# Attention of a two-layer transformer kernel: units of two heads in one sequence of ticks, scores 12 and 14 products behind the maxima

## The reference

```python
# layer 0 attention: 16 heads of 16, 4 key/value heads, band of +-64 tokens, a sink added to every score
att = einsum('bhqd,bhkd->bhqk', q, k) * 16 ** -0.5 + sink
att = softmax(where(|i - j| <= 64, att, -inf))
x = layernorm(x + (att @ v) @ wo)
x = layernorm(x + int8_ffn(x))                  # 256 -> 1024 -> 256
# layer 1 attention: 16 heads of 16, causal
att = softmax(where(j > i, -inf, q @ k.T * 0.25))
x = layernorm(x + (att @ v) @ w_out.T + b_out)
x = layernorm(x + moe(x))                       # 2 of 16 experts, and 2 shared ones
```

## Time and profile before

| what | us |
|---|---|
| median of 3 runs (lowest to highest) | 995.63 (992.62 to 998.64) |
| the profiled execution | 998.8 |
| its span, first to last instruction | 997.0 |
| PE busy | 827.6 (83%) |
| DVE, ACT, POOL busy | 555.6, 492.1, 348.5 |

### The profile page before, as it was taken

How to read it: one execution, slowest core, us unless ns; L and a number is a source line. 1 busy time by engine, 2 the same in 40 slices (tenths; PEclk the granted TensorE clock), 3 DMA queues, 4 the chain that set the end, 5 groups by cost and what they waited for, 6 DMA issues and landing times. The chain is left out here.

```text
span 997.0 us, 15493 instructions
## 1 busy us (share of the span) xinstructions
PE 827.6 (83%) x5521; PEld 641.7 (64%) x5534; DVE 555.6 (56%) x1381; ACT 492.1 (49%) x1064; POOL 348.5 (35%) x630
## 2 busy tenths in 40 slices
PE   6996999889789997988899889699984328999946
PEld 3775766577577566756756677477643318889935
DVE  5543478465337845814685473347825406688924
ACT  3373555745455475554447645355462106555503
POOL 6762502415341032344303326251141560045521
PEclk9697999979799997988999798799996658999978
DMA  8049000000000000000000000003323220045452
GB/s 225 2 26 247 1 1 2 2 1 24 1 1 1 2 2 1 3 23 0 1 2 2 1 2 2 1 1 136 127 52 80 74 99 20 17 139 155 139 201 84
DMA packets 34626, 47.27 MB, mean 47 GB/s; under 512 B 9948, under 2 KB 27998, under 8 KB 33688
## 3 DMA queue, kind: packets, MB, share of 16 engines
q1 hardware_dynamic: 25184, 20.29, 8.5%
q0 software_dynamic: 6656, 23.27, 7.3%
q10 hardware_dynamic: 2712, 2.73, 0.8%
HBM read 20.09 MB, written 18.69 MB: 39 GB/s over the span
## 5 line engine op out<-in xcount | busy, mean ns | idle before, releaser
L1033 DVE TENSOR_REDUCE negmax<-ps 128x2 fp32r<-128x512 f32 (+4 forms) x304 | 176.9, 628 | 45.0 <-PE ps L1347 42.5
L765 ACT ACTIVATE prob<-ps 128x448 f32<-128x448 f32 (+2 forms) x320 | 151.1, 524 | 57.5 <-PE ps L1360 55.0
L1347 PE MATMUL ps<-kT,qT 128*128 128x256 f32 (+4 forms) x512 | 150.8, 371 | 0.0
L1360 PE MATMUL ps<-qT,kT 128*128 128x192 f32 (+4 forms) x512 | 122.6, 328 | 10.2 <-ACT prob L765 4.7
L572 POOL TENSOR_TENSOR carry_p<-neg_half 128x1 f32<-128x1 f32 x80 | 16.4, 205 | 284.0 <-ACT prob L765 284.0
L1360 PEld LDWEIGHTS ps<-qT,kT 128*128 128x128 f32 x512 | 82.9, 198 | 47.3 <-ACT prob L765 32.5
L577 POOL TENSOR_SCALAR_AFFINE_SELECT prob<-prob 128x512 f32<-128x512 f32 (+1 forms) x192 | 110.1, 602 | 0.0
L1347 PEld LDWEIGHTS ps<-kT,qT 128*128 128x128 f32 x512 | 95.6, 200 | 3.0 <-issue 0.8
L1374 PE MATMUL ps<-prob,v_aug 128*32 128x256 f32 (+4 forms) x1024 | 77.7, 411 | 13.3 <-POOL prob L577 13.1
L902 DVE TENSOR_TENSOR xT<-ps,xT 128x256 fp32r<-128x256 f32 x96 | 39.4, 420 | 78.0 <-ACT xT L653 75.8
L616 POOL DMA_INDIRECT token_y<-ys_sb,y_row x47 | 45.1, 959 | 89.6 <-DVE ys_sb L1194 89.0
(11 more groups left out here) (206 smaller groups left out, 1835.8 us busy)
## 6 DMA issues: line engine op xcount, KB each, us to landing
xs_sb<-slot_x SPq DMA_DIRECT2D x47, 129.0 KB
slot_x<-zeros SPq DMA_DIRECT2D x1, 6016.0 KB, 33.2
w_sb<-in_w POOLq DMA_DIRECT2D x4, 1408.0 KB, 12.3
w_sb<-in_w POOLq DMA_DIRECT2D x5, 704.0 KB, 9.1
x_all<-in_x SPq DMA_DIRECT2D x4, 512.0 KB, 3.8
w_sb<-token_y SPq DMA_DIRECT2D x2, 1024.0 KB, 11.7
w_sb<-token_y ACTq DMA_DIRECT2D x2, 1024.0 KB, 12.6
out<-y_all SPq DMA_DIRECT2D x4, 512.0 KB, 2.9
```

The lines of the kernel that those rows point to most:

```text
L765: act.activation(prob[:, part % PROB_BUFS, j, 0:n], ps[:, 3 + i % 3, 0:n], ACT.Exp, scale=SCALE).then_inc(exped[l].sem, 1)
L1033: dve.tensor_reduce(out=negmax[:, t, s * GH + j * mh:s * GH + (j + 1) * mh], in_=ps[:, k % 3, 0:mh * n].rearrange("p (h n) -> p h n", n=n) ...
L1347: ins = pe.matmul(dst[:, jj, :], qT[:, h // 2, t * P:(t + 1) * P], kT[:, k_block(h), k0:k0 + n], start=False, stop=True, skip_group_check= ...
L1360: ins = pe.matmul(ps[:, 3 + item % 3, col:col + n], kT[:, k_block(h), kt * P:(kt + 1) * P], qT[:, h // 2, q0:q0 + n], start=True, stop=Tru ...
```

## The change

A unit of two heads (`UH = 2`, eight units) takes the place of the group of four. There are no slots: one sequence of ticks runs through the stage, and every step has the tick at which it stands worked out by a small function. Score item i stands at tick i + 12 in layer 0 and i + 14 in layer 1 (`SCORE_LAG`). The stage has 45 and 63 ticks instead of 48 and 72 places. Raw items are now 4 and 6 for a unit, so 32 and 48 for a stage: in layer 1 the item of four heads by 128 keys becomes two. The maxima are turned and sent once for a unit (8 times and not 4), and one DMA on SP carries both rows of a unit where two DMAs carried the four rows of a group. `pv_part` now has two heads and stands 6 score items back for odd units and 8 for even ones, so that the last part of an even unit and the first of the odd unit behind it have the same tick; the two units use different quarters of bank 6 (`c = 32 * (h % GH)`). `prob` has six buffers of two heads and not three of four, which is the same memory. `oT_copy`, `o_transposes` and `normalise` still go by four heads. POOL has 16 or 24 parts of two heads. The router input (`x3_tr`) stands at ticks 4 and 8, the router at tick 34, and the head steps of the next sequence at ticks 50, 52, ... 60.

The diff, cut to its core:

```diff
-PROB_BUFS = 3
+PROB_BUFS = 6
 PV_LAG = 6
 SHIFT_AT = 2
-MAX_HEADS = tuple([min(GH, 512 // query_tile_keys(l, t)[1]) for t in range(NT)] for l in (0, 1))
-MAX_ITEMS = tuple([(t, j) for t in range(NT) for j in range(GH // MAX_HEADS[l][t])] for l in (0, 1))
+NU, UH = 8, 2
+MAX_HEADS = tuple([min(UH, 512 // query_tile_keys(l, t)[1]) for t in range(NT)] for l in (0, 1))
+MAX_ITEMS = tuple([(t, j) for t in range(NT) for j in range(UH // MAX_HEADS[l][t])] for l in (0, 1))
+SCORE_LAG = (12, 14)
+X3_TICKS = (4, 8)
+def shift_tick(l, u):
+    return (u + 1) * len(MAX_ITEMS[l]) + SHIFT_AT
+def pv_tick(l, part):
+    n_parts = len(PARTS[l])
+    return UH * part + 1 + SCORE_LAG[l] + (PV_LAG if part // n_parts % 2 else PV_LAG + 2)
+def group_tick(l, g):
+    return pv_tick(l, (2 * g + 2) * len(PARTS[l]) - 1)
+def o_tick(l, g):
+    return group_tick(l, g) + (3, 4)[l]
+def head_tick(i):
+    return shift_tick(1, NU - 1) + 2 * i
+TICKS = tuple(NU * len(MAX_ITEMS[l]) + SCORE_LAG[l] + 1 for l in (0, 1))
...
-                        for parity in (0, 1):
-                            sp.dma_start(qT[STACK * parity + SHIFT:STACK * parity + SHIFT + 1, 2 * g:2 * g + 2, :].bitcast(F32),
-                                         shift_row[parity:GH:2, g % 2, :].bitcast(F32)).then_inc(sh_row[g][l].sem, 16)
+                        sp.dma_start(qT[SHIFT:P:STACK, u, :].bitcast(F32), shift_row[:, u % 2, :].bitcast(F32)).then_inc(sh_row[u][l].sem, 16)
...
-                                                             pattern=[[0, GH], [sign, hi_q - lo_q]], channel_multiplier=-sign)
+                                                         pattern=[[0, UH], [sign, hi_q - lo_q]], channel_multiplier=-sign)
...
-                    def pv_part(g, p):
-                        pe.wait_ge(*kept[l].at(b, g * n_parts + p + 1))
-                        if p == 0 and g >= 1:
-                            pe.wait_ge(*oT_out[l].at(b, g))
+                    def pv_part(part):
+                        u, p = divmod(part, n_parts)
+                        pe.wait_ge(*kept[l].at(b, part + 1))
+                        if p == 0 and u % 2 == 0 and u >= 2:
+                            pe.wait_ge(*oT_out[l].at(b, u // 2))
                         for i, (kt, off) in enumerate(PARTS[l][p]):
                             q0, n = key_tile_queries(l, kt)
-                            for j in range(GH):
-                                h = g * GH + j
-                                ins = pe.matmul(ps[32 * j:32 * j + 32, 6, q0:q0 + n],
+                            for j in range(UH):
+                                h = u * UH + j
+                                c = 32 * (h % GH)
+                                ins = pe.matmul(ps[c:c + 32, 6, q0:q0 + n],
...
-                            ins = pe.matmul(ps[0:GH, 7, t * P:(t + 1) * P], negmax[:, t, (s - 1) * GH:s * GH], ident_r[:],
+                            ins = pe.matmul(ps[0:UH, 7, t * P:(t + 1) * P], negmax[:, t, u * UH:(u + 1) * UH], ident_r[:],
...
-                    for s in range(NG + 2):
-                        g = s - 2
-                        if g >= 0:
-                            pe.wait_ge(*sh_row[g][l].at(b, 2 * 16))
-                        for i in range(max(n_items, n_parts * GH)):
-                            if g >= 0 and i < n_parts * GH:
-                                score_item(g, i)
-                            if s < NG and i < n_items:
-                                raw_item(s, i)
-                            if i == SHIFT_AT and 1 <= s <= NG:
-                                shift_tr(s)
+                    for k in range(TICKS[l]):
+                        if 0 <= k - SCORE_LAG[l] < NU * UH * n_parts:
+                            score_item(k - SCORE_LAG[l])
+                        if k < NU * n_items:
+                            raw_item(k)
+                        for u in range(NU):
+                            if k == shift_tick(l, u):
+                                shift_tr(u)
...
+                        for part in range(NU * n_parts):
+                            if k == pv_tick(l, part):
+                                pv_part(part)
+                        for g in range(NG - 1):
+                            if k == o_tick(l, g):
+                                o_transposes(g)
```

More of the change, by code:

```diff
@@ L217, in build @@
         scope.append(attn_scope)
-        prob = sb("prob", [P, PROB_BUFS, GH, 512])
+        prob = sb("prob", [P, PROB_BUFS, UH, 512])
         qkv_sb = sb("qkv_sb", [P, 6 * C])
@@ new lines, in batch @@
+                    n_parts = len(PARTS[l])
+                    for part in range(NU * n_parts):
+                        u, p = divmod(part, n_parts)
+                        buf = part % PROB_BUFS
+                        pool.wait_ge(*exped[l].at(b, (part + 1) * UH))
+                        c = (l * NU + u) * 3 + p
+                        pool.tensor_tensor(out=carry_p[:, c:c + 1], in0=neg_half[:], in1=neg_half[:], op=ALU.add)
+                        for kt, col in PARTS[l][p]:
+                            q0, n = key_tile_queries(l, kt)
+                            for lo_q, hi_q, base, sign in unseen(l, kt):
+                                sel = prob[:, buf, :, col + lo_q - q0:col + hi_q - q0]
+                                ins = pool.affine_select(out=sel, in_=sel, compare_op=ALU.is_ge, fill=0.0, base=base,
+                                                         pattern=[[0, UH], [sign, hi_q - lo_q]], channel_multiplier=-sign)
+                        ins.then_inc(kept[l].sem, 1)
+                        if l == 1 and not last:
+                            for i in range(HEAD_STEPS):
+                                if (head_tick(i) - SCORE_LAG[1]) // UH == part:
+                                    head_step(b + 1, i)
@@ new lines, in attention @@
+                    for k in range(TICKS[l] + 2):
+                        if k < NU * n_items:
+                            max_item(k)
+                        if l == 0 and b >= 1:
+                            for i in (0, 1):
+                                if k == X3_TICKS[i] + 1:
+                                    for t in (2 * i, 2 * i + 1):
+                                        split_lo(b - 1, "x3", t, bank0=4)
+                        for g in range(NG - 1):
+                            if k == o_tick(l, g) + 1:
+                                normalise(g)
+                        if l == 1 and not last:
+                            for i in range(HEAD_STEPS):
+                                if k == head_tick(i):
+                                    head_step(b + 1, i)
@@ L1383, in o_transposes @@
                             pe.wait_ge(*o_put[l].at(b, g))
+                        pe.wait_ge(*sh_out[l].at(b, sum(shift_tick(l, u) <= o_tick(l, g) for u in range(NU))))
                         for t in range(NT):
@@ L1441, in attention @@
+                    for part in range(NU * n_parts):
+                        if pv_tick(l, part) >= TICKS[l]:
+                            pv_part(part)
                     ahead = l == 1 and not last
```

201 lines of the change are left out of this document (87 added, 114 removed).

## The result

The median is **1026.26 us** (1024.95 to 1029.08) where the kernel before has 995.63: a ratio of 1.0305, 95% interval 1.0265 to 1.0345. The forecast was 1018, range 988 to 1042, own range 1008 to 1028. The profiled execution has a span of 1023.5 us (before 997.0), 26.5 more, where the sum said 22. PE's total and its main line come first; the columns of the group are busy us, mean ns, idle before and what ended it.

What follows compares the result with a forecast made beforehand. PE was taken to bound each attention stage's middle, and nearly its end. Layer 0's +4.6 and layer 1's +18 were rounded to +22 us: 998.8 profiled becomes 1021, median 1018; range 988 to 1042, own range 1008 to 1028.

Steps and rivals of the forecast that it cites:

- rival 4: Order tighter than its signals (bank 7, layer 1 row's DMA, POOL at the end): 1 to 2 us more a stage, 1030; chance 0.13.
- A pair costs what four cost: Value products on PE: two heads by 512 columns take 1.00 us, as four did; the line's 77.7 us about doubles.
- Rival 2: Every `pv_part`: a pair costs half of what four cost, so value products add nothing; 980 us, chance 0.10.
- Neighbours in one tick overlap: Even unit's last value part and odd unit's first: the shorter is hidden, 0.89 us a group in layer 0, 0.57 in layer 1.
- rival 1: Neighbouring value parts don't overlap: 23 us on top, 1041 us; chance 0.20.
- First part: Stage start with only raw items: shorter, 7.3 us (-2.4) in layer 0 and 7.2 us (-4.4) in layer 1.
- Third part and tail: Stage end: free PE time gained, 3.0 us in layer 1 and 3.2 in layer 0, less 0.8 there for a new wait.
- Rival 3: Gaps in the second and third parts are worth 1.5 to 2.5 us a stage more: about 1000 us; chance 0.20.
- The normalise wait at tick 30: Layer 0: the turning at tick 30 writes bank 7 and must wait for DVE's maximum 29 and `normalise`: 0.8 us.
- Router stages: Three layer 0 stages: -1.2 us for the first score's wait, +1.0 for less PE slack at a lower clock; +1.1 each in all.
- Layer 1, +5.1 a stage: Layer 1 stage sum: value products +8.0, turnings +0.7, first part -4.4, moved raw items +3.8, third part and tail -3.0 us.
- 4.5 as the mean of four: Layer 1's last stage has a first part 0.9 us longer but less free time at its end: mean 4.5 us, +18 in all.

Runs made afterwards that it cites:

- quads: Kernel after, with even units' value parts held back to the odd neighbour's so four heads stream together, 4 not 6 items behind in layer 1: 1000.63 us.
- own_tick: Kernel after, with all value parts of even units one tick earlier, so neighbouring units' parts don't share a tick: 1050.05 us.
- x3_before_late: Kernel before, with the router input's products between items of the first two slots and the expert weights' load after the last scores: 993.61 us.
- late_after: Kernel after, with the expert weights' load of the last sequence moved behind the last stage's scores: 1019.42 us.
- late_before: Kernel before, with the expert weights' load of the last sequence moved behind the last stage's scores: 993.91 us.

## Why the prediction was right, and where its size was off

The mechanism was right and with it the direction. The time came 8 us beyond the forecast, within its own range, but nearer to the 1030 of rival 4 than to 1018; and the 8 us are a sum of errors that partly cancel.

- **A pair costs what four cost.** Right: 0.99 us for a part, 122.7 us for the line (about 120). Rival 2 is gone by the trace, and quads shows it is the cause: 25.6 us come back.
- **Neighbours in one tick overlap.** Right: 1.00 us for both, and separated they cost +23.8 us where rival 1 put 23. That the two numbers meet is partly luck: 3.3 us of it are the new wait in layer 0, and the stages account for 19.8 us only.
- **Turnings.** 0.24 each, right.
- **First part.** In layer 1 6.68 where I had 7.2: -4.9 for -4.4, and no wait of 0.3 in the first seven stages. Layer 0: 6.8 for 7.3, so -2.9 for -2.4.
- **Third part and tail.** The 3.0 us that I took for layer 1 were free time of PE. Its visible idle there fell from 22.10 - 19.66 = 2.4 to 19.22 - 19.01 = 0.2 us; what short gaps gave besides can't be read. The lengths of the parts don't test the term, since ten score items moved from the third part into the middle. Rival 3 wanted 1.5 to 2.5 us more a stage, and the stages are longer than the sum, not shorter.
- **The normalise wait at tick 30: not in the trace.** PE's waits in the first stage are 0.4 us for POOL and 0.3 for ACT, none ahead of a turning. I had left out the value part of tick 29, which stands between `o_transposes` and the turning and covers it. In own_tick that part is one tick earlier, and there the turning waits 0.82 us. So this term was 0.8 too dear, the first part gave 0.5 more than I had, and yet the stage is +1.3 as forecast: 1.3 us of the other terms were too cheap. That the stage came out exactly is luck.
- **Router stages.** Forecast +1.1 each; measured -1.1, +1.0 and -0.9. The first score still waits 0.5 us for the router's input, so 0.7 was won and not 1.2. The rest is the clock: in the kernel before it was at the lower level for 6.8, 3.4 and 6.9 us in the third parts of these stages, in the kernel after for 3.4 in each. A stretch of 6.8 us costs 2.7 (20.1 against 17.4 us for the third part in two router stages of x3_before_late), so the 6.9 us less of it make an estimated 2.7 of the 4.3 by which layer 0 came in low. With a third part at full clock in both orders the term holds: the one such stage of late_after takes 42.1 us, its counterpart in late_before 41.1.
- **Layer 1, +5.1 a stage.** Measured +5.8. Behind the first part the stage grew by 10.7 us, where the terms make 8.0 + 0.7 + 3.8 - 3.0 = 9.5. Which of them was 1.2 too small, no experiment shows.
- **The last stage, "4.5 as the mean of four": the step that failed.** I took the row's 3.0 us from turning to first score, read from the first stage, for all eight stages and put 0.3 us for the wait. In the eighth a load of 6.49 MB is under way: 718.67 - 710.69 = 7.98 us from turning to first score, 5.30 of it idle, and 1.8 us more at a lower clock. late_after takes both away and gives back 6.8 us of median. Rival 4 names the row (6 ticks where it had 10), but as 1 to 2 us in every stage; it was 7 in one. The row of the kernel before at 706.38, idle 0.74, was the sign that I did not read. Counting ticks from there would not have been enough: four ticks of 0.53 us less give a wait of 2.9 us, and it was 5.3, since an earlier row didn't come earlier. The wait is the end of the load, 12 us into the stage, less the 6.7 us of the new first part.

The sum for the spans closes, with the forecast before rounding: 4.6 + 18 = 22.6, and 22.6 - 4.3 (layer 0) + 11.3 (layer 1) - 3.1 (rest) = 26.5, as measured (it was rounded to 22 where 23 was due). The median moved 30.6; it lies 3.2 below the profiled execution before and 1 above it after, which is the scatter of single executions.

## What to carry to other kernels

Where several small products stream side by side, the price is that of the longest, so count streams per pass before you make units smaller: halving the heads of a unit doubles the passes, and the shorter ends did not pay for that here (a stage of layer 1 had 8.0 us more of passes by my sum, and 5.8 were left as loss). A single sequence of ticks was worth 0.7 to 1.1% with the units left at four. When a transfer loses slack, look up its latency in every stage, above all in the one where a bulk load starts, and ask when that load ends: issuing the transfer earlier may not bring it earlier.

## What the runs showed of the hardware that was not expected

- A transfer of 4 KB issued on SP's queue is delayed by a bulk load issued on POOL's: 6.93 us from issue to the score that waits for it, 4.10 in the kernel before (702.28 to 706.38, under the same load), and 2.50 in the first stage, without it. Its own packets move only when nearly all of the 6.49 MB are through, so that the product that needs it starts at the same distance from the load, 11.8 to 12.5 us into the stage in nine kernels, whether the row was issued at 5.1 or at 8.4 us.
- With an idle of 5.30 us on PE comes a stretch at the lower of its two clock levels (1.2 for 2.4 GHz), which begins before the idle ends: the middle's mean clock is 0.94 and it is 1.76 us longer. The other layer 1 stages, with waits of 0.2 us, have it at 1.00.
- Two value products in different quarters of the columns, one behind the other in the program, start 0.007 us apart, although each runs in two passes and the second pass of 512 columns starts 0.45 us behind the first (162.08 and 162.53 in the kernel before).
- Router stages at full clock and with part of them at 1.2 GHz differ by 1.2 to 3.1 us (42.2 to 44.4 in the kernel before, 41.0 to 41.3 with the late load), and where the clock falls changes between kernels whose work in that stretch is the same.
